# Attention and spline feed-forward on one core: the order of weight products and loads in the first feed-forward batch

## The reference, cut

```python
xn = layernorm(x)                                   # x: 4 x 512 x 512
q, k, v = (heads(xn @ W + b) for W, b in ...)       # 16 heads of 32
scores = q @ k.T / sqrt(32) + alibi                 # causal
attn = softmax(scores) @ v @ Wo + bo
gate_w, up_w = spline(gate_cp), spline(up_cp)       # 2048 x 512, Catmull-Rom in 8134 control points
down_w = spline(down_cp)                            # 512 x 2048
ffn = (silu(xn @ gate_w.T) * (xn @ up_w.T)) @ down_w.T
out = x + attn + ffn
```

## Time and profile before

| what | us |
|---|---|
| runs shown, median (lowest, highest) | 775.7 (773.27, 783.23) |
| profiled execution, own time | 774.91 |
| its span | 773.1 |
| PE busy | 679.8 (88%) |
| DVE busy | 457.9 (59%) |
| ACT busy | 445.4 (58%) |
| POOL busy | 330.7 (43%) |
| mean granted clock of PE | 0.971 |

### The profile page before, as it was taken

One profiled execution on the slowest core, in us unless ns is written; L12 is line 12 of the kernel. 1 busy time (PEld: TensorE's weight loads), 2 busy tenths in 40 slices (PEclk: granted clock), 3 DMA queues, 4 the chain that ended last, 5 costly groups with the idle time before them and its releaser, 6 DMA issues.

```text
span 773.1 us, 13681 instructions
## 1 busy us (share of the span) xinstructions
PE 679.8 (88%) x4884; PEld 543.3 (70%) x4884; DVE 457.9 (59%) x1290; ACT 445.4 (58%) x705; POOL 330.7 (43%) x191
## 2 busy tenths in 40 slices
PE   4978779989789898799898777788979999999997
PEld 3756657777567776578776565566758888888885
DVE  6287867879857878768799686665323213223122
ACT  4388867877857878677879663444322333232331
POOL 1565554555535545444546430322125236335334
PEclk9998999999899999999999999899989999999999
DMA  7986377475765375672946937859248475243101
GB/s 246 163 184 119 54 225 134 62 135 158 125 163 82 43 123 111 138 150 42 206 82 96 365 109 256 269 134 281 60 141 253 129 233 179 88 121 126 39 1 54
DMA packets 53067, 109.75 MB, mean 142 GB/s; under 512 B 6408, under 2 KB 6664, under 8 KB 51464
## 3 DMA queue, kind: packets, MB, share of 16 engines
q1 hardware_dynamic: 51416, 106.46, 56.1%
q10 hardware_dynamic: 1584, 2.43, 1.2%
HBM read 59.32 MB, written 25.17 MB: 109 GB/s over the span
## 4 chain that ended last, share of the span: by engine, by line
PE 39%; DVE 5%; issue 4%; POOL 3%; ACT 3%; DMA 2%; ACTq 1%; SPq 0%; POOLq 0%; DVEq 0%
PE bank L1471 6%; PE bank L1472 6%; PE bank L1473 6%; PE bank L1458 3%; PE bank L1459 3%; PE bank L583 2%; PE bank L638 2%; PE bank L585 2%; POOL resid L1625 2%; PE bank L584 2%; DMA bm_early<-bases_scratch 2%; PE bank L624 1%; DVE w_new L1569 1%; ACTq L365 1%; ACT w_new L1509 1%
## 5 line engine op out<-in xcount | busy, mean ns | idle before, releaser
L1153 POOL TENSOR_TENSOR work<-work 128x1280 f16<-128x1280 f32 x64 | 171.1, 2673 | 176.5 <-ACT work L1050 176.5
L1617 POOL TENSOR_TENSOR in_lo<-inner,in_hi 128x512 fp32r<-128x512 f32 x64 | 85.2, 1333 | 202.8 <-ACT in_hi L1535 202.8
L830 DVE CUSTOM_DVE_ANT_0 work<-bank,dist 128x128 f32<-128x128 f32 (+3 forms) x256 | 115.4, 487 | 78.8 <-PE bank L624 61.7
L1042 ACT ACTIVATE work<-work,neg_max 128x128 f32<-128x128 f32 (+3 forms) x256 | 130.1, 562 | 18.4 <-DVE neg_max L830 18.2
L1535 ACT CAST in_hi<-inner 128x512 fp32r<-128x512 f32 x64 | 39.8, 622 | 147.1 <-PE bank L1473 141.1
L1581 DVE TENSOR_TENSOR inner<-bank,silu 128x512 f32<-128x512 f32 x64 | 44.1, 689 | 132.5 <-ACT silu L1529 125.1
L638 PE MATMUL bank<-ident,work 128*128 128x128 f16 x1280 | 105.2, 226 | 10.3 <-DVE work L839 8.3
L1050 ACT CAST work<-work 128x1280 f16<-128x1280 f32 x64 | 80.7, 1260 | 55.3 <-PE bank L638 54.7
L638 PEld LDWEIGHTS bank<-ident,work 128*128 128x128 f16 x1280 | 75.4, 101 | 46.8 <-issue 33.3
L1471 PE MATMUL bank<-w_room,in_hi 128*128 128x512 f32 x256 | 101.4, 396 | 0.5 <-POOL in_lo L1617 0.5
L1472 PE MATMUL bank<-w_room,in_hi 128*128 128x512 f32 x256 | 101.0, 395 | 0.0
(11 more groups left out here) (100 smaller groups left out, 1300.7 us busy)
## 6 DMA issues: line engine op xcount, KB each, us to landing
q_stack<-parts SPq DMA_DIRECT2D x48, 256.0 KB, 5.7
k_stack<-parts SPq DMA_DIRECT2D x48, 256.0 KB, 6.1
z<-xt_scratch SPq DMA_DIRECT2D x128, 88.0 KB
x_in<-x SPq DMA_DIRECT2D x32, 256.0 KB, 4.1
xt_scratch<-xt_room SPq DMA_DIRECT2D x8, 1024.0 KB, 6.7
xt_room<-xt_scratch SPq DMA_DIRECT2D x6, 1024.0 KB, 9.9
factor<-c_basis SPq DMA_DIRECT2D x5, 1024.0 KB, 9.3
taps<-windows SPq DMA_DIRECT2D x5, 1024.0 KB, 11.1
```

What stands on the lines that cost most here:

```text
L830: dve.tensor_tensor_reduce(probs[:, s % 2, OFF[i]:OFF[i] + n], score_bank[i % 2][:, 0:n], dist[:, S - n:S], -slope(s), 3.4e38, ALU.add, AL ...
L1042: e = act.activation(tile, tile, ACT.Exp, bias=neg_max[:, s % 2, i:i + 1], scale=-1.0)
L1153: pool.tensor_tensor(probs16[:, s % 2, 1, :], probs[:, s % 2, :], probs16[:, s % 2, 0, :], ALU.subtract).then_inc(lo_ready, 1)
L1617: pool.tensor_tensor(in_lo[k % 2][:, :], inner[:, k % 2, :], in_hi[:, k % 2, :].bitcast(F32), ALU.subtract).then_inc(il_ready, 1)
```

## The change

In the first batch of the feed-forward, PE's order of a step becomes gate/up, gen, down (it was gate/up, down, gen). The two moment products for the second batch move from behind tiles 11 and 13 to behind tiles 8 and 10, and since gen now stands earlier in the step they follow the down product directly. On SP, the early basis goes ahead of chunk 1; windows 4 to 7 and their moments are issued at the end of attention, ahead of the stores of the sums, behind a wait for the last value product (`av_full`); pieces 3 go behind the later windows, the basis and the rows of the next batch. ACT's first moment eviction waits for the stores of the sums, since its buffer lies over theirs.

```diff
         sp.wait_ge(pj_full, pj_total(("k", KC - 1), B - 1))
+        load_basis(sp)
         load_chunk(sp, 1)
-        load_basis(sp)
         load_chunk(sp, 2)
...
         load_moments(sp, 0, 0)
         load_pieces(sp, 1)
+        sp.wait_ge(av_full, H * B)
+        for g in range(4, 8):
+            load_windows(sp, 0, g)
+        load_moments(sp, 0, 1)
         for q in range(QT):
             store_sum(B - 1, q)
...
+        if t == 0 and g + 2 < NG:
+            order.append(("gen", g + 2, 0, 1))
         if k >= LAG:
             order.append(("down", k - LAG, 0, None))
-        if t == 0 and g + 2 < NG:
-            order.append(("gen", g + 2, 0, 1))
-        if t < B - 1 and g in ((11, 13) if t == 0 else (6, 8)):
-            half = 0 if g == (11 if t == 0 else 6) else 1
+        if t < B - 1 and g in ((8, 10) if t == 0 else (6, 8)):
+            half = 0 if g == (8 if t == 0 else 6) else 1
...
                 act.wait_ge(mom_full, n - 2)
+                if n == 3:
+                    for q in range(QT):
+                        act.wait_ge(res_st[q], 16 * B)
...
         sp.dma_start(factor[3][:], c_factor[3]).then_inc(chunk_ld[3], 16)
-        for g in range(4, 8):
-            load_windows(0, g)
-        load_moments(0, 1)
         sp.dma_start(taps[4][:], cpts[4]).then_inc(chunk_ld[4], 16)
...
         load_moments(0, 2)
-        load_pieces(3)
         for g in range(12, NG):
             load_windows(0, g)
         load_moments(0, 3)
         sp.dma_start(bm[:].bitcast(F32).rearrange("p k e n -> p (k e n)"), moment_d).then_inc(bm_ld, 16)
         load_xt(1)
+        load_pieces(3)
         sp.wait_ge(made[4], 4)
```

## The result

The changed kernel takes 790.0 us (median), the kernel before 775.3 beside it: ratio 1.0173, interval 1.0123 to 1.0223. One of its four executions took 3657.8 us and is not in the ratio; the median of the other three is 788.8. The forecast was 793, with a range of 780 to 800. The profiled execution took 788.8 us, its span is 787.0.

A forecast was written before the change was run, and what follows sets the result against it. PE was taken to bound the first feed-forward batch, with a few waits. From 774.9 us: basis -3.6, steps +13.0, clock +10.9, moments -2.9 gave 792.3; with 0.8 for the median, 793, range 780 to 800.

The forecast's parts named there:

- The chain over ACT's cast: In plain first-batch steps, 2.24 us from gate/up's start to the weight product through ACT and DVE; step 6.02 instead of 4.55.
- The waits for made weights: PE's waits before weight products in the first feed-forward batch: near 28 us in sum instead of 7.2.
- the second rival: First batch: the weight product finds its banks free, so the kernel gets faster, 757 us; chance 0.06.
- the first: Rival for the first batch: the clock holds through PE's gaps, median 782 us; chance 0.18.
- the fourth: Rival at the early basis: it gains nothing, DVE's wait for chunk 1 replaces PE's, 797 us; chance 0.06.
- The steps with more on ACT: Steps 6 and 10 of the first feed-forward batch, where ACT issues four copies across (2.83 us): 8.85 each before moments.
- the 99.7: Forecast time from gate/up 2 to 16 in the first batch, without slow clock: 99.7 us against 86.7, +13.0.
- The clock: Slow clock behind four first-batch gaps of 3.5 us or more (9.2) and two of 2.2 to 2.6 (1.7): +10.9 us.
- the third rival: First batch: the clock swings in plain steps too, seven more drops at 1.7 us, 805 us; chance 0.10.
- The basis: Early basis ahead of chunk 1: PE's 3.74 us wait goes, DVE's next maximum starts sooner, -3.6 us.
- The moments asked for sooner: Moment products behind tiles 8 and 10: the 3.65 us wait at gate/up 16 and its slow stretch go, -2.9 us.
- Rows 4 to 7 and pieces 3: SP's reordered loads, rows 4 to 7 ahead of the sums' stores and pieces 3 behind basis and rows: 0.

The follow-up runs named there:

- Experiment 1: Changed kernel with PE's old first-batch order (gate/up, down, gen) and moment products behind tiles 11 and 13 again, moved loads kept: 771.6 us, ratio 0.9936.
- experiment 2: Changed kernel with only gen put back behind the down product; moments stay behind tiles 8 and 10, moved loads stay: 765.8 us, ratio 0.987.
- 4 (ACT): Changed kernel with ACT's copy out of the weight banks ahead of its cast to in_hi in the first batch: 761.4 us, ratio 0.98.
- experiment 3: Kernel before with only gen put ahead of the down product; moments and loads as before: 799.5 us, ratio 1.0302.
- experiment 6: Changed kernel with the early basis loaded behind chunk 1 again: 792.2 us, ratio 1.0202.
- experiment 5: Changed kernel with DVE's first multiply on chunk 1 put one head later: 788.1 us, ratio 1.0152.

## Why the prediction was right, and by how much each step was off

*The chain over ACT's cast* was forecast at 2.24 us and a plain step at 6.02; the steps measure 6.01 to 6.05. Experiments 1 and 2 (order) and 4 (ACT) show that it is the cause, by undoing it from either end, and experiment 3 by making it alone. The waits for made weights, forecast near 28 us, come to 23.7 (22.7 and 1.0 in the rows above); the copies of the next point are 1.6 of the difference. With the chain in every step the second rival falls, with the four slow stretches the first, and with the shorter stretch to gate/up 2 the fourth, by little more than the spread (see the basis).

*The steps with more on ACT.* The weight product of steps 6 and 10 starts 4.26 us after gate/up, not 5.07. This is ACT in step 6:

```profile
518.70 0.62 ACT L1542 CAST in_hi<-inner 128x512 fp32r<-128x512 f32 x1 [4.53 <-PE bank L1477]
518.72 0.47 ACTq L365 DMA_DIRECT2D wgu_hi<-wgu_hi  x1
...
521.25 0.58 ACT L1516 COPY w_new<-bank 128x512 f32<-128x512 f32 x1 [1.93 <-issue]
```

The forecast set 0.53 from the cast to the next instruction and then the 2.83 of the earlier trace rows for the copies. Here the first copy is issued 0.02 us after the cast has started, and ACT's copy out of the banks starts 2.53 after that: 2.55 in place of 3.36. Two times 0.8 comes off the 99.7, which leaves 98.1 at full clock.

*The clock* was the term most off: 10.9 forecast, about 7.1 measured (105.2 less 98.1). Four drops came, in steps 2, 5, 6 and 8, at 1.6 to 2.2 us each. I had counted six, four at 2.3 and two at 0.85; those of step 10 and of the second moment product stayed out, 3.15 of the 3.8. The gap of 3.19 in step 10 left the clock at 1.00, while that of 3.17 in step 6 did not, and the slow stretch around step 2 began before the gap to which I put it down. So the length of a gap, by which I forecast, did not pick out the gaps that cost; what does is not shown. The plain gaps cost nothing, as the earlier trace rows had it. So the third rival falls, and with it the rule of the Trainium skill (TensorE: Matmul & The Clock Gate, A second HAM failure mode: psum-queue depth-cycling) as I had applied it here: 43 us with seven gaps of 0.5 to 3.2 us ran at 1.00.

*The basis* gave 2.9 us up to gate/up 2, 3.6 was forecast. The chunk did land where the basis had, and DVE waited for it; but the multiply took 1.39 us, not 0.69. By experiment 6 the swap itself is 1.6 to 2 of it. The rest is no more than the spread of this stretch: experiment 3, with the instructions of the kernel before up to gate/up 2, took 74.0 where that kernel took 74.9.

*The moments asked for sooner* gave 2.3 us behind gate/up 16, 2.9 was forecast; experiment 2 against 1 puts the whole of it, with the wait, at 5.8 by the medians and 6.6 by the traces.

*Rows 4 to 7 and pieces 3* were forecast at 0. Experiment 1 holds them with the basis: 771.6 against 775.1, about what the basis and the shorter wait at gate/up 16 give. No run has them alone.

The sum in spans is +13.9 against +17.4 forecast. The copies were put 1.6 too high and the clock 3.8; the gains at the basis and behind gate/up 16 came out 1.3 smaller than forecast; and 0.8 is a difference ahead of the first changed instruction, which no forecast has. So the mechanism was right. The terms are off by 7.5 us in all and the total by 3.5, because their errors partly cancel.

## What to carry to other kernels

Before you move work forward on one engine, follow the buffer that it needs back through the in-order queues of the others: what matters is not when the result could be ready, but which instruction, waiting for what, stands ahead of the one that frees the buffer. Here a copy behind a cast that waits for the down product turned an order meant to help into a loss of 24 us, and swapping the two on ACT took the changed kernel from 788.8 us to 761.4, below the kernel before (775.1 beside it). A wait taken off one queue should be followed on the queue that receives it: on SP it held stores that PE needed.

## What the runs showed of the hardware

A DVE multiply of two 128x512 operands took 0.68 us alone and 1.39 when POOL had a subtraction under way as it started; this is POOL's timeline of the changed kernel, beside the multiply at 434.70:

```profile
432.94 2.61 POOL L1153 TENSOR_TENSOR work<-work 128x1280 f16<-128x1280 f32 x1 [1.88 <-ACT work L1050]
```

The multiply ends at 436.09, about 0.5 after POOL's 435.55: it looks as if it waited for POOL and then ran. In experiment 5, too, the two multiplies (439.47 to 443.17) end about 0.6 after POOL (442.62). Where the multiply starts first it is POOL that takes longer: the multiply at 388.95 in the changed kernel takes 0.68, and POOL's subtraction from 389.19 on 2.93 instead of 2.61. The Trainium skill (SBUF — State Buffer, SBUF: two separate sides) says that DVE operations with two inputs in SBUF and GpSimd operations that read SBUF lock a shared pair of ports for a whole instruction, and the later one blocks; these rows agree with that.

And a gap's length alone did not decide the clock: 3.17 and 3.19 us in two like steps, a drop behind one and none behind the other. In experiment 3 the gap of step 10 was 3.18, and the clock fell behind it (0.67). What makes the difference is not settled here.
